# Splitting a weight unit on GpSimd one token iteration later, with the last hidden split moved into the next stage

## What is computed

```
h  = einsum('bct,bcd->bdt', x, cond_weights[itok_B_1_198])
x  = x + attention(h)            # 16 heads, 8 kv heads, rope, top-k keys by a routing gate, Wo
h2 = x @ W.T + lora(x)[adapter]  # "cond2": a 512x512 projection and a rank-16 adapter
Wg, Wu, Wd = dequant_nvfp4(...)  # 4-bit codes by a table, times a scale for 32 values; 4096 wide
x  = x + (gelu(h2 @ Wg.T) * (h2 @ Wu.T)) @ Wd.T
```

## Time and profile before

| | us |
|---|---|
| Median of three runs | 2833.7 (2833.45 to 2834.11) |
| Profiled execution, its own time | 2834.1 |
| Its span in the trace | 2832.5 |
| PE busy | 2675.9 (94%) |
| DVE busy | 2179.6 (77%) |
| ACT busy | 1227.1 (43%) |
| POOL busy | 988.2 (35%) |
| Token stage, to the first FFN product | 792.17 |

### The profile page before, as it was taken

The page is one execution under the profiler, slowest core; times in us unless marked ns, Lnnn a source line. Parts: engine busy times, 40 slices in busy tenths (PEclk is TensorE's granted clock), DMA queues, the critical chain, the costliest instruction groups (busy, mean ns, idle before and its releaser), DMA issues.

```text
span 2832.5 us, 54312 instructions
## 1 busy us (share of the span) xinstructions
PE 2675.9 (94%) x19200; PEld 2458.1 (87%) x19200; DVE 2179.6 (77%) x3724; ACT 1227.1 (43%) x2425; POOL 988.2 (35%) x1189
## 2 busy tenths in 40 slices
PE   5888889888789999999999999999999999999998
PEld 4787878787689999999999999999999999999998
DVE  6677777778758888888888888888888888755555
ACT  3444445454334444444444444444444444444443
POOL 3334433443623443534433442534333443300000
PEclk7999999999899999999999999999999999999999
DMA  3123232322576687669667865976686687657452
GB/s 118 61 77 107 79 103 72 102 83 84 207 293 226 232 296 303 234 228 364 244 230 262 337 242 205 346 257 255 242 330 228 250 301 275 229 211 294 182 193 92
DMA packets 197576, 599.87 MB, mean 212 GB/s; under 512 B 21224, under 2 KB 80488, under 8 KB 185200
## 3 DMA queue, kind: packets, MB, share of 16 engines
q1 hardware_dynamic: 162160, 496.89, 48.1%
q0 software_dynamic: 35328, 101.82, 9.6%
HBM read 417.83 MB, written 180.75 MB: 211 GB/s over the span
## 4 chain that ended last, share of the span: by engine, by line
PE 79%; DVE 14%; issue 3%; ACT 2%; DMA 1%; SPq 0%; DVEq 0%; ACTq 0%
PE bank_a L879 22%; PE down L887 22%; PE proj L709 13%; PE bank_b L879 12%; PE bank_c L879 6%; PE scores L749 2%; DVE inter L1426 2%; DVE inter L1417 1%; DVE lut_line L1213 1%; PE scores L758 1%; DVE inter_parts L1433 1%; DVE rope_in L1259 1%; ACT inter L1128 1%; DVE hs L1240 1%; PE pv L774 1%
## 5 line engine op out<-in xcount | busy, mean ns | idle before, releaser
L879 PEld LDWEIGHTS bank_a<-h_in,gu_slot 128*128 128x128 f32 x6144 | 855.9, 190 | 76.6 <-ACT copy_p L1148 7.6
L879 PE MATMUL bank_a<-h_in,gu_slot 128*128 128x256 f32 x6144 | 899.0, 282 | 8.5 <-ACT copy_p L1148 7.4
L887 PE MATMUL down<-d_slot,inter_parts 128*128 128x512 f32 x3072 | 835.5, 394 | 2.0 <-DVE inter_parts L1433 2.0
L887 PEld LDWEIGHTS down<-d_slot,inter_parts 128*128 128x128 f32 x3072 | 527.6, 190 | 68.6 <-DVE inter_parts L1433 2.4
L879 PE MATMUL bank_b<-h_in,gu_slot 128*128 128x256 f32 x3072 | 456.3, 284 | 16.4 <-DVE up_val L1439 16.4
L592 POOL TENSOR_TENSOR lut_v<-lut_v,signed_scale 128x512 f32<-128x512 f32 x96 | 123.5, 1286 | 956.7 <-DVE lut_v L1229 956.6
L879 PEld LDWEIGHTS bank_b<-h_in,gu_slot 128*128 128x128 f32 x3072 | 404.6, 192 | 23.7 <-DVE up_val L1439 23.7
L1164 ACT ACTIVATE gate_val<-bank_a 128x256 f32<-128x256 f32 x256 | 98.1, 383 | 429.3 <-PE bank_a L879 429.3
L1413 DVE TENSOR_TENSOR up_val<-bank_b,copy_p 128x256 f32<-128x256 f32 x256 | 108.2, 423 | 204.5 <-PE bank_b L879 204.4
L1433 DVE TENSOR_TENSOR inter_parts<-inter,inter_parts 128x512 fp32r<-128x512 f32 x256 | 202.7, 792 | 33.7 <-ACT inter_parts L1132 33.7
L879 PE MATMUL bank_c<-h_in,gu_slot 128*128 128x256 f32 x1536 | 226.0, 283 | 0.0
(11 more groups left out here) (123 smaller groups left out, 3716.6 us busy)
## 6 DMA issues: line engine op xcount, KB each, us to landing
h_in<-h_scratch SPq DMA_DIRECT2D x64, 3584.0 KB, 12.8
acc<-out SPq DMA_DIRECT2D x64, 1024.0 KB, 5.4
out<-acc SPq DMA_DIRECT2D x64, 1024.0 KB, 4.3
gu_slot<-w_scratch SPq DMA_DIRECT2D x32, 1792.0 KB, 10.3
w_scratch<-w_parts POOLq DMA_DIRECT2D x96, 512.0 KB, 6.9
h_scratch<-h_out SPq DMA_DIRECT2D x32, 896.0 KB, 5.0
d_scratch<-w_parts POOLq DMA_DIRECT2D x32, 512.0 KB, 3.7
d_slot<-d_scratch SPq DMA_DIRECT2D x32, 512.0 KB, 15.8
```

The costliest lines, as they stand in the source:

```text
L879: ins = pe.matmul(bank[:, 0:HALF], lhsT, rhs, start=(start and n == 0), stop=(n == len(pairs) - 1), skip_group_check=True)
L887: ins = pe.matmul(down[tc][:].rearrange("p (k h) -> p k h", k=2), inter_parts[:, j % 2, u, tc * P:(tc + 1) * P], d_slot[j][:, :, v, :], st ...
```

## The change

`SLOTS` now has two units in iterations 0 and 1 and one in each later iteration, so iteration t from 2 on makes unit t + 2 of the eighteen. On POOL the store of an iteration's last unit moves into the next iteration, right behind its residual sum; where there are two units, the first is stored behind `k_low` and the second is scaled there. The combines now stand in iterations 2, 4, 8, 10 and 14, and the last one behind the last `spread`. In the FFN's first two steps ACT and DVE split the two halves of iteration 15, each behind the second copy of its step, and SP issues the `d_slot` loads ahead of their stores.

```diff
-        SLOTS = [1 if t < NT - 2 else 2 for t in range(NT)]
+        SLOTS = [2 if t < 2 else 1 for t in range(NT)]
...
             load_gate_up(0, 3)
-            store_hidden(NT - 1, 0)
-            store_hidden(NT - 1, 1)
             evacuated(sp, BEHIND, "h3")
             for j in range(NS):
                 load_down(0, j)
+            store_hidden(NT - 1, 0)
+            store_hidden(NT - 1, 1)
...
                 ins.then_inc(residual_ready, 1)
+                if t > 0:
+                    store_unit(*UNITS[t - 1][-1])
                 if t + MIXES < NT:
                     gather(t + MIXES)
                 scale_unit(*UNITS[t][0])
...
+                if len(UNITS[t]) > 1:
+                    store_unit(*UNITS[t][0])
+                    scale_unit(*UNITS[t][1])
                 if t > 0:
                     spread(t, t - 1, 1)
                 if t < NT - 1:
                     q_low(t + 1)
-                store_unit(*UNITS[t][0])
-                for c, k in UNITS[t][1:]:
-                    scale_unit(c, k)
-                    store_unit(c, k)
...
             spread(BEHIND, NT - 1, 1)
+            store_unit(*UNITS[NT - 1][-1])
...
-            hidden_high(NT - 1, 0)
-            hidden_high(NT - 1, 1)
...
                         inter_high(n - 1, 1 - b)
+                    if first and j < 2:
+                        hidden_high(NT - 1, j)
                     act.wait_ge(p5_full, n + 1)
...
-            hidden_low(NT - 1, 0)
-            hidden_low(NT - 1, 1)
...
                         inter_low(n - 1, 1 - b)
+                    if first and j < 2:
+                        hidden_low(NT - 1, j)
                     up_from_s3(n)
```

## The result

The changed kernel takes **2809.99 us** (median of four runs, 2806.93 to 2816.62) against 2833.57 of the kernel before: ratio 0.992, 95% interval 0.99 to 0.994. Run again later beside three variants it took 2812.24 (2809.61 to 2816.75), ratio 0.9933 (0.992 to 0.9945). The forecast was 2822 with a range of 2806 to 2836: the direction and the range hold, and the forecast change is too small, by 12 us by the medians and 9.8 by the spans. The profiled execution of after took 2812.71 with a span of 2811.1, against 2834.1 and 2832.5: **21.4 us less in the span**.

A forecast was written before the change was run, and what follows sets the result against it. PE was taken to bound the FFN and nearly the token stage, so POOL changes win only where PE waits. Middle +0.9, iterations 0 and 1 +0.5, iteration 15 -13, FFN start 0: -11.6 from 2833.7, giving 2822 us, range 2806 to 2836.

The forecast's parts named there:

- Iteration 15, -13: Last token iteration: early residual sum lets h_in0 load 13.7 us earlier, so PE turns at 765 instead of 778.1.
- The boundaries, 0.9 less: Iteration starts: without a store behind q_low, PE's 1.68 us wait becomes 0.8, giving 42.66 us per iteration.
- Light stores, 0.6 each, with 6.6 for clock falls: Mid-iteration: a store without combine delays DVE's unit steps, 0.6 us reaching PE (bounds 0 to 1.3); other clock falls total 6.6.
- Combines in the middle, 4.7 each: Iterations 2, 4, 8, 10, 14: POOL's combine delays DVE and lowers PE's clock, adding 4.7 us each (bounds 1 to 9).
- the walk: Mid-iteration beside a combine: strict DVE and POOL alternation, five DVE waits totalling 4.2 us, 3.8 reaching PE at turn_probs.
- The Trainium skill's rule that was weighed against the walk: Shared ports locked per whole instruction: DVE gets a turn after POOL's first, each combine holding it 0.7 us less, 3.5 total.
- Iterations 0 and 1, +0.5: First two iterations with doubled units: last lookup step waits about 3 us for a store, mostly slack; +0.5, between 0 and 4.
- The FFN's start, 0: First FFN steps: 7.39 us stall goes, but h_in1 lands later, second tile near F + 35; 0, between -3 and +4.
- the one in which the combines hide: Mid-iteration: DVE mostly gets its turn first, a combine adds 1 to 2 us, middle gives 15: 2807 us; chance 0.14.
- the tail gains nothing: Iteration 15: early loads meet h2 stores and POOL's loads, the store lands as late relatively: 2834 us; chance 0.12.
- The third rival: Mid-iterations: residual sum stays bound by x1's store, light stores cost the boundary's 0.9; middle +10, 2831 us; chance 0.10.
- The slower rival: Mid-iterations: DVE's last lookup step waits for a stretched combine; at 10 us each, middle +27, 2849 us; chance 0.10.

The follow-up runs named there:

- the two kernels with the rest of the combine elsewhere: Changed kernel with stores behind spread 1, each combine's last combination and store behind the next residual sum (2795.55 us) or behind q_low (2797.67 us).
- the kernel with the place alone: Kernel before, two units still in iterations 14 and 15, but each iteration's last unit stored behind the next residual sum: 2825.99 us, ratio 0.9967.

## Why the prediction was right and where it was not

- **Iteration 15, -13:** right in size (-13.0), and in the steps up to the load: the residual sum at 728.85, `h_in0` issued 10.1 us after the value product (733.3), landed after 17.5 us, no 8.44 us gap. The kernel with the slots alone shows it by itself. The last steps went otherwise. The h2 store was to land 33.4 us after the value product and to be what is late last, with the turn 3.4 behind it. It landed at 31.2 (issued at 749.42, 5.0 us), ScalarE did not wait for it (755.00), and PE turned 5.3 us later, at the end of its own chain (3.37 us of waiting for the probabilities at 744.32, 0.94 at 755.98). That the two differences cancel is luck.
- **The boundaries, 0.9 less:** right. The rope step is at 0.69 and PE's wait at 0.79, and with the light stores elsewhere an iteration takes 42.67 to 42.80 where 42.66 was worked out. One reading beside it was wrong, and nothing rests on it: the residual sum in the earlier trace rows was not 13.1 us late, which is its distance from the combine's first instruction. It starts 12.4 us behind the value product where ordinary iterations have it at 5.3 to 6.5, so it was 6 to 7 late.
- **Light stores, 0.6 each, with 6.6 for clock falls:** nine iterations were to take 9 x 43.26 + 6.6 = 395.9 us and take 394.5 (the six at a clock of 1.00 have a mean of 43.34, the three at 0.96 of 44.83). The forecast lies inside the 394.5 to 399.1 of the four executions with this middle. The mean of 0.6 is right; that it is 0.2 in one iteration and 1.4 in another was foreseen in the bounds, by their reason too. Iteration 1 is among the nine and carries its second unit: 45.45 us against 44.21 before, both at 0.96.
- **Combines in the middle, 4.7 each:** the term that was mis-sized. Five iterations were to take 5 x 47.96 = 239.8 and take 235.7: **3.9 each**, 4.1 us in all (3.5 to 3.9 in the four executions). The step that failed is the walk. It had VectorE lose 4.2 us ahead of `turn_probs` and PE wait 3.8 there, and PE waits 1.02 in iteration 4. Of its five waits (0.5, 0.6, 1.3, 0.5, 1.3) the trace has 0.2, 0, 0.4, 0 and 1.1: the unit steps and L1308 are late by 1.7 together (0.45, 0.70 and 2.30 instead of 0.28, 0.28 and 1.21), and the low rank part and one unit step passed without a wait. The walk had nothing behind that, and PE waits 1.2 more than usual for the routing product, 1.9 and 2.1 more in iterations 2 and 8. The Trainium skill's rule that was weighed against the walk (SBUF — State Buffer, "SBUF: two separate sides") would have taken 3.5 us off, and the measured middle lies nearer to that; but VectorE's first unit step met only the second of the two combinations here, so these rows don't settle whether it gets a turn between them. The combine without its arithmetic sets the price at 3.0.
- **Turn to F, -2.5:** missing from the sum. I counted the stall as 8.44 us and nothing behind it, though for the waits in the middle I did count the clock. The same 77 matmuls take 14.06 us at a granted clock of 0.74 and 11.55 at 1.00; the kernel with the split alone, which keeps the stall, has 13.46 at 0.78. But the stall isn't all of it. The slots alone, the middle without combine arithmetic and the two kernels with the rest of the combine elsewhere have no stall there and take 12.84 to 13.07 at 0.87. The stretch of the one with the rest behind the residual sum, its products behind the turn, and the same products in the changed kernel:

```profile
742.46:755.50 13.04, 11.06 (x76) 10.66 (x77) 1.54 (x3) 2.12 (x5) 1.77 (x4) 0.87 0.97 364
744.61 2.80 PE L722 MATMUL proj<-x1T,wa 128*128 128x256 f32 x12 [1.50 <-DVE x1T L1329]
761.88 1.66 PE L711 MATMUL proj<-x1T,wa 128*128 128x256 f32 x12 [1.50 <-DVE x1T L1318]
```

The wait is the same, and the clock behind it isn't. So 1.0 to 1.2 of the 2.5 us go with the stall, and for the rest the cause is not shown.
- **Iterations 0 and 1, +0.5:** -0.7 up to the value product of iteration 1. It can't be read: the same program run twice had that product at 93.06 and 89.97.
- **The FFN's start, 0:** right (-0.5), and nearly all of its steps: second tile forecast at F + 35 and seen at F + 35.03; second h2 store at F + 16 (787.6 is F + 16.3), and PE ends its wait with the landing of `h_in1`. The landing of that store was F + 23, two late, and `h_in1` took 12.0 us, one less than the lower bound.
- **The sum:** the parts of the miss are -4.1, -1.4, -2.5, -1.2 and -0.5, together -9.7 of the 9.8 us between -11.6 and -21.4.

Of the rivals, the one in which the combines hide has a time (2807) that is nearer to the measured one than the forecast's, and its reason (VectorE gets its turn more often) is half right. But it had 15 us from the middle, where 4.7 came; part of its closeness is the clock behind the turn, of which it says nothing. That the tail gains nothing is refuted, but the kernel with the reordered SyncE shows how most of a gain there can be lost again. The third rival's condition is met: the residual sum waits for the landing of x1's store in every iteration (4.3 to 7.2 us), and in iterations 5 and 11 a light store costs 1.4 and 1.2, more than the boundary gives. In the mean it is 0.7, so the rival's time (2831) is not. The slower rival's wait was seen once, in the kernel with the place alone, in iteration 15.

What stays open: why the clock stays at 1.00 in one iteration and falls in another after the same wait of 1.45 us (or of 1.50 behind the last turn), from kernel to kernel and between executions of one kernel; and the 1.9 us behind F in the kernel with the slots alone.

## What to carry to other kernels

Work moved off one boundary costs where it lands, by what the other engines do there: the same combine cost 3.5 to 4 us beside a dense row of VectorE steps, 2.6 in most cases in a stretch in which VectorE had small steps and GpSimd stood still, and 0.3 to 0.9 where the clock stayed at 1.00 once the part that did not fit into that stretch was cut off and put elsewhere. Look for the longest wait of the engine that carries the movable work and fit the pieces to it. A store of under 1 MB that somebody waits for should not be issued behind a load of 3.5 MB; here swapping the two only moved the wait, and issuing the load earlier removed it. And when a stall of 8 us goes, look at the stretch behind it too: its matmuls were busy a quarter longer (12.08 us against 9.57). Not all of that need come back, since in four kernels without the stall they were busy for 10.9 to 11.1.

## What was not expected of the hardware

- The granted clock fell after PE's usual 1.45 us wait in iterations without any disturbance (0.96, 44.2 us) in one kernel, and did not fall in another (1.00, 42.7 us). It differs between executions of the same program too: iterations 6 and 7 of the changed kernel took 43.05 and 42.88 at 1.00, and 44.63 and 44.39 at 0.96 when it was run again.
- Behind the 8.44 us stall 77 matmuls took 14.06 us, without it 11.55 in five kernels and 12.84 to 13.07 in four.
- The store of a weight part (512 KB) held GpSimd for 9.36 us while `h_in0` was loading; the h2 stores (896 KB) land in 5.0 us in iteration 15 of the changed kernel and took 14.62 behind that load in the earlier trace rows.
